# Softmax sums taken in the first pass over the scores, the logarithm folded into the second, eight heads to a mix

## The chip, the cores and the metric

The kernel runs on one core of a Trainium2 chip. The metric is the device time of one execution in microseconds. TensorE (PE) multiplies matrices, VectorE (DVE), ScalarE (ACT) and GpSimd (POOL) do elementwise work, SyncE (SP) issues transfers. PE writes its results to PSUM, eight banks of 512 float32 columns on 128 partitions; POOL reads and writes only SBUF.

## The reference, cut to what matters

A transformer layer on 16 items of 256 tokens and 512 features, all in float32: self-attention, cross-attention to a context of the same size, and a feed-forward part with 2048 hidden features. Each part starts with a layer norm whose scale and shift are computed from `cond`.

```python
def _attn(q, k, v):                       # 16 heads of 32 features, 256 queries, 256 keys
    scores = einsum('bqhd,bkhd->bhqk', q, k) * 32 ** -0.5
    out = einsum('bhqk,bkhd->bqhd', softmax(scores), v)
    return out.reshape(B, Lq, 512)
x = x + _attn(rope(q1), rope(k1), v1) @ sa_out_w.T      # q1, k1, v1 from adaln(x)
x = x + _attn(rope(q2), rope(k2), v2) @ ca_out_w.T      # q2 from adaln(x), k2, v2 from context
x = x + (gelu(adaln(x) @ ffn_w1.T + b1) @ ffn_w2.T + b2)
```

`rope` turns each pair of features (t1, t2) into (t1 cos - t2 sin, t2 cos + t1 sin).

## The kernel before

Accuracy is kept by splitting each float32 operand of a projection into a high part and a low part (`w_hi`, `w_lo`; `xx_hi`, `xx_lo`; `o_hi`, `o_lo`) and summing three products. ACT makes the high part by a copy, DVE or POOL subtracts to get the low part.

The two attention layers are one stage of 32 items (16 of self-attention, 16 of cross-attention), each of 16 heads, so 512 heads in a row; the feed-forward part is a second stage. The order of the attention stage is written out by hand in `stage_order`: `put(place, step)` gives every step a place, three places to a head, and every engine walks through the same list and does the steps that are its own. PE, ACT, DVE, POOL and SP therefore each work strictly in that order, and wait on semaphores for each other.

For every head n the list has two passes, eight heads (`LAG`) apart:

- `scores`: PE multiplies q by k into a bank of `ps_s` (L603, two products of 256 queries x 256 keys in halves of 128 queries), and DVE takes the negative maximum of each query over the keys (L851). Then the bank is free.
- `max_split`, `max_turn`, `max_copy`, once per four heads: DVE splits the maxima of four heads in a high and a low part (L859, L862), PE turns them by a product with the identity (L612), and ACT copies them into eight extra rows of `qT` (L729).
- `weigh`: PE computes the scores once more, transposed (keys on the partitions), with the negative maxima added by the extra rows (L623), ACT takes the exponential with the scale 32 ** -0.5 into `prob` (L737), and POOL adds the two halves of the keys into `sums_sb` (L908).
- `mix`, once per four heads (a "quad"): PE multiplies v by `prob` into the left half of the bank `ps_o` (L636) and a matrix of ones by `sums_sb` into its right half (L643), so that every row holds the softmax sum. `invert` (ACT, L744 and L746) turns the sum into its inverse by a logarithm and an exponential, `divide` (DVE, L867) multiplies, `o_split` (ACT, L753) and `o_low` (POOL, L896) split the result for the output projection.

Between these stand the projections of the items ahead, about two units per head: `project` (L589, L593), the turning of x with its modulation on ACT (`turn_x`, L692), and rope: DVE multiplies by cos (L822) and sin (L826), POOL adds (L902), ACT makes the high part (L722) and DVE the low part (`rope_low`, L843), and SP sends both through memory into the stacked layout of `qT` and `kT`.

`ps_s` has four banks, taken in turn by all steps of the kinds `scores`, `weigh` and `max_turn` in the order of the list (`score_users`); a step waits until the user four turns before it has been read (`scores_left`). `ps_g` has three banks and `ps_o` one. `prob` has room for six heads (`NP`).

## Time and profile before

| | |
|---|---|
| median of three runs | 1990.77 us (1989.99 to 1994.31) |
| span of the profiled execution | 1991.3 us |
| PE busy in the span | 1955.2 us, 98% |
| ACT busy | 1221.5 us, 61% |
| DVE busy | 1335.1 us, 67% |
| POOL busy | 1097.4 us, 55% |
| attention stage | up to about 1306 us |

The profiled execution has a time only as its span; it lies among the three timed runs, so the span is used as its own time. A row of a group names line, engine, operation, output<-input, shape and count, then the busy time in us and the mean ns of one, then the engine's idle time just before. Idle time of an engine that is not the bound costs nothing. Busy time counts overlapping instructions of an engine once; the mean ns is an instruction's whole length.

### The profile page before, as it was taken

What the parts mean: (1) busy time and instruction counts of PE and PEld (TensorE: products, weight loads), DVE (VectorE), ACT (ScalarE), POOL (GpSimd) and SP (SyncE); (2) the same over time, 40 slices, a digit from 0 to 9 for tenths busy, and PEclk for the clock granted to TensorE, in tenths of its full rate; (3) what the DMA queues carried; (4) which work ended last, traced back from release to release, by engine and by line L of the source; (5) the groups of instructions that cost most, each with busy time, mean ns of one, the idle gap of its engine ahead of it and who ended that gap; (6) DMA issues with size and microseconds to landing.
All of it is one profiled execution on the core that took longest, in us unless ns stands there. A gap on an engine that the chain in (4) does not pass through costs nothing. (4 is left out here: it accounts for less than half of the span.)

```text
span 1991.3 us, 40759 instructions
## 1 busy us (share of the span) xinstructions
PE 1955.2 (98%) x14612; PEld 1666.6 (84%) x14612; DVE 1335.1 (67%) x2317; ACT 1221.5 (61%) x2277; POOL 1097.4 (55%) x1205
## 2 busy tenths in 40 slices
PE   7999999999999999999999999899999999999999
PEld 6788888888887888888888887678998989989998
DVE  6866776776677676666667666545676676666654
ACT  3565566666666666666666666655656666666654
POOL 2555566566666676766666676523444363553531
PEclk9999999999999999999999999999999999999999
DMA  7877667676778686667667676543322323232230
GB/s 245 219 203 182 173 172 193 162 192 177 179 196 224 174 222 192 180 192 207 186 173 206 190 180 177 152 133 97 115 82 78 107 64 96 85 95 88 63 96 32
DMA packets 300197, 307.53 MB, mean 154 GB/s; under 512 B 15840, under 2 KB 253664, under 8 KB 300000
## 3 DMA queue, kind: packets, MB, share of 16 engines
q1 hardware_dynamic: 299408, 304.45, 55.4%
q8 instruction: 121, 1.98, 0.4%
q14 instruction: 76, 0.62, 0.1%
q10 hardware_dynamic: 592, 0.47, 0.1%
HBM read 212.59 MB, written 92.27 MB: 153 GB/s over the span
## 5 line engine op out<-in xcount | busy, mean ns | idle before, releaser
L908 POOL TENSOR_TENSOR sums_sb<-prob 128x256 f32<-128x256 f32 x512 | 405.1, 796 | 323.1 <-ACT prob L737 321.8
L851 DVE TENSOR_REDUCE neg_max<-ps_s 128x2 f32<-128x512 f32 x512 | 347.7, 686 | 335.2 <-PE ps_s L603 332.8
L737 ACT ACTIVATE prob<-ps_s 128x512 f32<-128x512 f32 x512 | 304.6, 596 | 348.6 <-PE ps_s L623 343.3
L902 POOL TENSOR_TENSOR rope_c<-rope_c,rope_s 128x512 f32<-128x512 f32 x128 | 179.0, 1398 | 115.9 <-DVE rope_s L826 115.1
L603 PE MATMUL ps_s<-kT,qT 96*128 96x256 f32 x1024 | 225.0, 301 | 2.3 <-DMA qT<-q_turned 2.3
L603 PEld LDWEIGHTS ps_s<-kT,qT 96*128 96x128 f32 x1024 | 164.5, 190 | 65.5 <-issue 53.9
L623 PE MATMUL ps_s<-qT,kT 104*128 104x256 f32 x1024 | 207.7, 284 | 10.0 <-ACT qT L729 7.2
L593 PE MATMUL ps_g<-xx_hi,w_hi 128*128 128x256 f32 x1024 | 210.4, 287 | 3.4 <-DVE rope_s L826 2.0
L593 PE MATMUL ps_g<-xx_hi,w_lo 128*128 128x256 f32 x1024 | 205.4, 282 | 0.0
L593 PE MATMUL ps_g<-xx_lo,w_hi 128*128 128x256 f32 x1024 | 204.8, 281 | 0.0
L1266 PE MATMUL ps_y<-w_hi,h_hi 128*128 128x512 f32 x512 | 201.5, 393 | 1.2 <-DVE h_lo L1391 1.2
L623 PEld LDWEIGHTS ps_s<-qT,kT 104*128 104x128 f32 x1024 | 170.6, 190 | 36.4 <-ACT qT L729 13.9
L1266 PE MATMUL ps_y<-w_lo,h_hi 128*128 128x512 f32 x512 | 200.6, 392 | 0.0
L1266 PE MATMUL ps_y<-w_hi,h_lo 128*128 128x512 f32 x512 | 199.4, 389 | 0.0
L1391 DVE TENSOR_TENSOR h_lo<-h_sb,h_hi 128x512 fp32r<-128x512 f32 x128 | 111.2, 872 | 103.7 <-ACT h_hi L1289 102.4
L1250 PE MATMUL ps_h<-xf_hi,cw_hi 128*128 128x256 f32 x592 | 167.4, 283 | 0.0
L1250 PE MATMUL ps_h<-xf_lo,cw_hi 128*128 128x256 f32 x592 | 165.8, 280 | 0.0
L1250 PE MATMUL ps_h<-xf_hi,cw_lo 128*128 128x256 f32 x592 | 165.7, 280 | 0.0
L593 PEld LDWEIGHTS ps_g<-xx_hi,w_hi 128*128 128x128 f32 x1024 | 158.4, 190 | 8.5 <-issue 5.2
L593 PEld LDWEIGHTS ps_g<-xx_lo,w_hi 128*128 128x128 f32 x1024 | 158.7, 191 | 0.0
L593 PEld LDWEIGHTS ps_g<-xx_hi,w_lo 128*128 128x128 f32 x1024 | 158.0, 190 | 0.0
L729 ACT ACTIVATE qT<-ps_s 8x1024 fp32r<-8x1024 f32 x128 | 130.4, 1018 | 3.1
(157 smaller groups left out, 4823.7 us busy)
## 6 DMA issues: line engine op xcount, KB each, us to landing
kT<-k_turned SPq DMA_DIRECT2D x192, 256.0 KB, 4.8
qT<-q_turned SPq DMA_DIRECT2D x64, 512.0 KB, 7.0
f_raw<-in_w1T SPq DMA_DIRECT2D x124, 256.0 KB, 3.1
k_turned<-rot_hi SPq DMA_DIRECT2D x64, 256.0 KB, 4.2
k_turned<-rot_lo SPq DMA_DIRECT2D x64, 256.0 KB, 4.3
q_turned<-rot_hi SPq DMA_DIRECT2D x64, 256.0 KB, 2.5
q_turned<-rot_lo SPq DMA_DIRECT2D x64, 256.0 KB, 2.6
qT<-q_turned SPq DMA_DIRECT2D x64, 256.0 KB, 7.5
```

The source lines that it names most:

```text
L593: ins = eng.matmul(ps_g[:, b, s * L:(s + 1) * L], w[:, row, (T * s + t) * P:(T * s + t + 1) * P], a[:, c, :], start=c == 0 and j == 0 and ...
L603: ins = eng.matmul(ps_s[:, score_bank(step), t * L:(t + 1) * L], qT[0:ROWS, G % NG, j, t * P:(t + 1) * P], kT[0:ROWS, G % NG, j, :], start ...
L623: ins = eng.matmul(ps_s[:, score_bank(step), t * L:(t + 1) * L], kT[:, G % NG, j, t * P:(t + 1) * P], qT[:, G % NG, j, :], start=True, sto ...
L729: eng.activation(qT[ROWS:MROWS, G % NG, OH * half:OH * (half + 1), :], ps_s[ROWS:MROWS, score_bank(step), 0:L].unsqueeze(1).broadcast_to([ ...
L737: eng.activation(prob[:, n % NP, :, :].rearrange("p t l -> p (t l)"), ps_s[:, score_bank(step), :], ACT.Exp, scale=HD ** -0.5).then_inc(ex ...
L851: eng.tensor_reduce(neg_max[G % 2][:, :, j], ps_s[:, score_bank(step), :].rearrange("p (t l) -> p t l", l=L), AX.X, ALU.max, negate=True). ...
L902: eng.tensor_tensor(rope_c[n % 2][:, :, :], rope_c[n % 2][:, :, :], rope_s[:, :, :], ALU.add).then_inc(rope_added, 1)
L908: eng.tensor_tensor(sums_sb[:, n % NP, :], prob[:, n % NP, 0, :], prob[:, n % NP, 1, :], ALU.add).then_inc(halves_added, 1)
L1250: ins = eng.matmul(ps_h[:, bank(p, n), 0:L], w[:, cols], x_[:, k, :], start=n in OPENS and k == 0 and j == 0, stop=k == 1 and j == 2, skip ...
L1266: ins = eng.matmul(ps_y[:, t, :], h[:, t * P:(t + 1) * P], w, start=c == 0 and j == 0, stop=c == FC - 1 and j == 2)
L1391: eng.tensor_tensor(h_lo[a % NH][:, :], h_sb[a % 2][:, :], h_hi[a % NH][:, :].bitcast(F32), ALU.subtract).then_inc(h_lo_done, 1)
```

## The change

The softmax sum is no longer taken from the second pass. A new ACT step `total` follows the maximum in the first pass: two exponentials of 128x256 (one for each half of the queries), read and written in place in the bank of `ps_s`, each with the negative maximum as a per-partition bias and with its sum over the keys written to `total`. The bank stays taken until they are done. Once per four heads ACT takes the logarithm of the sums (`log`), and DVE subtracts it from the negative maxima before it splits them (`max_split`, which now waits for `log` and stands three places later), so that the second pass gives normalized weights. The ones product, `sums_sb`, `invert` and `divide` are gone. A mix takes eight heads and one bank of `ps_s`, of which there are now five; `ps_o` is gone. `o_split` and `o_low` work once per eight heads on 128x512 and read that bank, so `o_low` moves from POOL to DVE. `rope_low` moves from DVE to POOL, and POOL's addition in rope becomes a subtraction and an addition of 128x256. The scale 32 ** -0.5 is put into the tables of cos and sin. `prob` has room for ten heads. Some projections, the store and the last items' steps move by one to five places. The modulation of x (L692) and the copies of the maxima (L729) are left as they are, on ACT.

```diff
-            late = {N: 24, N + 1: 14}.get(ahead, 0)
+            late = {N: 26, N + 1: 14}.get(ahead, 0)
...
-                turns(shares((p + 29, 6, k[:4]), (p + 45, 7, k[4:])))
+                turns(shares((p + 29, 6, k[:4]), (p + 46, 7, k[4:])))
...
-                    spread(p + 45, 7, v)
+                    spread(p + 46, 7, v)
...
-                    shares((p + 29, 6, v[:4]), (p + 45, 7, v[4:]))
+                    shares((p + 29, 6, v[:4]), (p + 46, 7, v[4:]))
...
-                turns(spread(p + 52, 14, q))
+                turns(spread(p + 53, 13, q))
...
-            spread(p + 36, 9, [("project", "o", i - 1, t, c) for cs in (range(KC - 1), (KC - 1,)) for t in range(T) for c in cs])
-            put(p + 47, "store", i - 1)
+            spread(p + 37, 9, [("project", "o", i - 1, t, c) for cs in (range(KC - 1), (KC - 1,)) for t in range(T) for c in cs])
+            put(p + 48, "store", i - 1)
...
-                spread(p + (58, 66, 78)[c], 6, [("project", "o", i, t, c) for t in range(T)])
+                spread(p + (58, 66, 83)[c], 6, [("project", "o", i, t, c) for t in range(T)])
...
         for half in range(2):
-            put(24 * G + 12 * half + 10, "max_split", G, half)
+            put(24 * G + 12 * half + 12, "log", G, half)
+            put(24 * G + 12 * half + 13, "max_split", G, half)
             put(24 * G + 12 * half + 19, "max_turn", G, half)
             put(24 * G + 12 * half + 20, "max_copy", G, half)
         if G:
             put(24 * G - 20, "stack", "k", G)
             put(24 * G - 17, "stack", "q", G)
 
-    for quad in range(4 * N):
-        place = 3 * (4 * quad + LAG + 5) + 2
-        for n, kind in enumerate(("mix", "invert", "divide", "o_split", "o_low")):
-            put(place + 2 * n, kind, quad)
+    for G in range(2 * N):
+        place = 3 * (8 * G + LAG + 9) + 2
+        for n, kind in enumerate(("mix", "o_split", "o_low")):
+            put(place + n, kind, G)
...
+            if part == 2 and n < HEADS:
+                yield ("total", n)
             for step in places.pop(3 * n + part, ()):
...
-    score_users = [step for step in order if step[0] in ("scores", "weigh", "max_turn")]
+    score_users = [step for step in order if step[0] in ("scores", "weigh", "max_turn", "mix")]
     score_turn = {step: n for n, step in enumerate(score_users)}
-    NS = 4
+    NS = 5
...
             cos_sb = sb("cos_sb", [P, L])
             pick_sb = sb("pick_sb", [P, OH])
...
@@ -375,14 +378,14 @@
             NV = 3
             v_sb = [sb(f"v_sb{n}", [P, T, D]) if n == (N_ITEMS - 1) % NV else v_kept[(N_ITEMS - 2 - n) % NV == 0] for n in range(NV)]
             neg_max = [sb(f"neg_max{n}", [P, T, HG]) for n in range(2)]
+            total = [sb(f"total{n}", [P, T, HG]) for n in range(2)]
+            log_sb = [sb(f"log_sb{n}", [P, T, OH]) for n in range(2)]
...
 
             max_parts = sb("max_parts", [P, T, MROWS])
-            NP = 6
+            NP = 10
             prob = sb("prob", [P, NP, T, L])
-            sums_sb = sb("sums_sb", [P, NP, L])
-            ones = sb("ones", [P, HD])
-
-            o_sb = sb("o_sb", [P, L])
+
             o_hi = sb("o_hi", [P, KC, L], F32R)
...
-                return {"scores": max_done, "weigh": exp_done, "max_turn": maxes_copied}[old[0]], nth[old]
+                return {"scores": total_done, "weigh": exp_done, "max_turn": maxes_copied, "mix": o_lo_done}[old[0]], nth[old]
...
                     elif kind == "mix":
-                        quad = step[1]
-                        i, c = divmod(quad, KC)
-                        eng.wait_ge(exp_done, OH * (quad + 1))
-                        if c == 0:
+                        G = step[1]
+                        i, g = divmod(G, 2)
+                        b = score_bank(step)
+                        eng.wait_ge(exp_done, HG * (G + 1))
+                        if g == 0:
                             eng.wait_ge(v_done, values[i, 1])
-                        if quad:
-                            eng.wait_ge(o_divided, quad)
-                        for k in range(T):
-                            for j in range(OH):
-                                ins = eng.matmul(ps_o[j * HD:(j + 1) * HD, 0, 0:L],
-                                                 v_sb[i % NV][:, k, c * P + j * HD:c * P + (j + 1) * HD],
-                                                 prob[:, (OH * quad + j) % NP, k, :], start=k == 0, stop=k == T - 1)
-                        if quad == 0:
-                            eng.wait_ge(ones_set, 1)
-                        eng.wait_ge(halves_added, OH * (quad + 1))
-                        for j in range(OH):
-                            ins = eng.matmul(ps_o[j * HD:(j + 1) * HD, 0, L:2 * L], ones[:, :],
-                                             sums_sb[:, (OH * quad + j) % NP, :], start=True, stop=True)
-                        ins.then_inc(mix_done, 1)
+                        for c in (2 * g, 2 * g + 1):
+                            cols = slice((c % 2) * L, (c % 2 + 1) * L)
+                            for k in range(T):
+                                for j in range(OH):
+                                    n = OH * (KC * i + c) + j
+                                    ins = eng.matmul(ps_s[j * HD:(j + 1) * HD, b, cols],
+                                                     v_sb[i % NV][:, k, c * P + j * HD:c * P + (j + 1) * HD],
+                                                     prob[:, n % NP, k, :], start=k == 0, stop=k == T - 1)
+                            ins.then_inc(mix_done, 1)
...
+                    elif kind == "total":
+                        n = step[1]
+                        G, j = divmod(n, HG)
+                        eng.wait_ge(max_done, n + 1)
+                        if j == 0 and G >= 2:
+                            eng.wait_ge(log_done, 2 * (G - 1))
+                        scores = ps_s[:, score_bank(("scores", n)), :]
+                        for t in range(T):
+                            ins = eng.activation(scores[:, t * L:(t + 1) * L], scores[:, t * L:(t + 1) * L], ACT.Exp,
+                                                 bias=neg_max[G % 2][:, t, j:j + 1], accum_out=total[G % 2][:, t, j:j + 1])
+                        ins.then_inc(total_done, 1)
+                    elif kind == "log":
+                        G, half = step[1:]
+                        eng.wait_ge(total_done, HG * G + OH * (half + 1))
+                        if nth[step] > 2:
+                            eng.wait_ge(shift_done, nth[step] - 2)
+                        eng.activation(log_sb[half][:, :, :], total[G % 2][:, :, OH * half:OH * (half + 1)], ACT.Ln).then_inc(log_done, 1)
                     elif kind == "weigh":
                         n = step[1]
                         eng.wait_ge(weigh_done, n + 1)
                         if n >= NP:
                             eng.wait_ge(mix_done, (n - NP) // OH + 1)
-                        eng.activation(prob[:, n % NP, :, :].rearrange("p t l -> p (t l)"), ps_s[:, score_bank(step), :], ACT.Exp,
-                                       scale=HD ** -0.5).then_inc(exp_done, 1)
-                    elif kind == "invert":
-                        quad = step[1]
-                        eng.wait_ge(mix_done, quad + 1)
-                        if quad:
-                            eng.wait_ge(o_lo_done, quad)
-                        eng.activation(o_sb[:, :], ps_o[:, 0, L:2 * L], ACT.Ln).then_inc(log_done, 1)
-                        eng.wait_ge(log_done, quad + 1)
-                        eng.activation(o_sb[:, :], o_sb[:, :], ACT.Exp, scale=-1.0).then_inc(den_inverted, 1)
+                        eng.activation(prob[:, n % NP, :, :].rearrange("p t l -> p (t l)"), ps_s[:, score_bank(step), :],
+                                       ACT.Exp).then_inc(exp_done, 1)
                     elif kind == "o_split":
-                        quad = step[1]
-                        i, c = divmod(quad, KC)
-                        eng.wait_ge(o_divided, quad + 1)
-                        if i and c == 0:
+                        G = step[1]
+                        i, g = divmod(G, 2)
+                        eng.wait_ge(mix_done, 2 * (G + 1))
+                        if i and g == 0:
                             eng.wait_ge(product_done, products["o", i - 1, 1])
-                        eng.activation(o_hi[:, c, :], o_sb[:, :], ACT.Copy).then_inc(o_hi_done, 1)
+                        eng.activation(o_hi[:, 2 * g:2 * g + 2, :], ps_s[:, score_bank(("mix", G)), :].rearrange("p (c l) -> p c l", l=L),
+                                       ACT.Copy).then_inc(o_hi_done, 1)
...
-                        eng.tensor_tensor(rope_s[:, :, :], pair[:, ::-1, :], sin_sb[:, :, :], ALU.mult).then_inc(rope_taken, 1)
+                        eng.tensor_tensor(rope_s[:, :, :], pair[:, ::-1, :], sin_sb[:, :].unsqueeze(1).broadcast_to([P, 2, L]),
+                                          ALU.mult).then_inc(rope_taken, 1)
...
-                    elif kind == "rope_low":
-                        n = ropes[step[1:]]
-                        if n > NT:
-                            eng.wait_ge(*rot_free(n))
-                        eng.wait_ge(rot_hi_done, n)
-                        eng.tensor_tensor(rot_lo[:, n % NT, :, :], rope_c[n % 2][:, :, :],
-                                          rot_hi[:, n % NT, :, :].bitcast(F32), ALU.subtract).then_inc(rot_lo_done, 1)
                     elif kind == "scores":
                         n = step[1]
                         G, j = divmod(n, HG)
@@ -855,19 +856,23 @@
                         eng.wait_ge(max_done, HG * G + OH * (half + 1))
                         if nth[step] > 1:
                             eng.wait_ge(max_turned, nth[step] - 1)
+                        eng.wait_ge(log_done, nth[step])
                         mine = neg_max[G % 2][:, :, OH * half:OH * (half + 1)]
-                        eng.tensor_reduce(max_parts[:, :, ROWS:ROWS + OH].bitcast(F32R), mine.unsqueeze(3), AX.X,
+                        eng.tensor_tensor(shift[:, :, :], mine, log_sb[half][:, :, :], ALU.subtract).then_inc(shift_done, 1)
+                        eng.wait_ge(shift_done, nth[step])
+                        eng.tensor_reduce(max_parts[:, :, ROWS:ROWS + OH].bitcast(F32R), shift[:, :, :].unsqueeze(3), AX.X,
                                           ALU.max).then_inc(max_hi_done, 1)
                         eng.wait_ge(max_hi_done, nth[step])
-                        eng.tensor_tensor(max_parts[:, :, ROWS + OH:MROWS], mine, max_parts[:, :, ROWS:ROWS + OH],
+                        eng.tensor_tensor(max_parts[:, :, ROWS + OH:MROWS], shift[:, :, :], max_parts[:, :, ROWS:ROWS + OH],
                                           ALU.subtract).then_inc(max_split, 1)
-                    elif kind == "divide":
-                        quad = step[1]
-                        eng.wait_ge(den_inverted, quad + 1)
-                        eng.tensor_tensor(o_sb[:, :], ps_o[:, 0, 0:L], o_sb[:, :], ALU.mult).then_inc(o_divided, 1)
+                    elif kind == "o_low":
+                        G = step[1]
+                        eng.wait_ge(o_hi_done, G + 1)
+                        chunks = slice(2 * (G % 2), 2 * (G % 2) + 2)
+                        eng.tensor_tensor(o_lo[:, chunks, :], ps_s[:, score_bank(("mix", G)), :].rearrange("p (c l) -> p c l", l=L),
+                                          o_hi[:, chunks, :].bitcast(F32), ALU.subtract).then_inc(o_lo_done, 1)
...
-                    elif kind == "o_low":
-                        quad = step[1]
-                        eng.wait_ge(o_hi_done, quad + 1)
-                        eng.tensor_tensor(o_lo[:, quad % KC, :], o_sb[:, :], o_hi[:, quad % KC, :].bitcast(F32),
-                                          ALU.subtract).then_inc(o_lo_done, 1)
                     elif kind == "project" and step[1] in "qk" and step[4] == KC - 1:
                         n = ropes[step[1:4]]
                         eng.wait_ge(cos_done, n)
                         eng.wait_ge(rope_taken, n)
-                        eng.tensor_tensor(rope_c[n % 2][:, :, :], rope_c[n % 2][:, :, :], rope_s[:, :, :], ALU.add).then_inc(rope_added, 1)
-                    elif kind == "weigh":
-                        n = step[1]
-                        eng.wait_ge(exp_done, n + 1)
-                        if n >= NP:
-                            eng.wait_ge(mix_done, (n - NP) // OH + 1)
-                        eng.tensor_tensor(sums_sb[:, n % NP, :], prob[:, n % NP, 0, :], prob[:, n % NP, 1, :],
-                                          ALU.add).then_inc(halves_added, 1)
+                        eng.tensor_tensor(rope_c[n % 2][:, 0, :], rope_c[n % 2][:, 0, :], rope_s[:, 0, :], ALU.subtract)
+                        eng.tensor_tensor(rope_c[n % 2][:, 1, :], rope_c[n % 2][:, 1, :], rope_s[:, 1, :], ALU.add).then_inc(rope_added, 1)
+                    elif kind == "rope_low":
+                        n = ropes[step[1:]]
+                        if n > NT:
+                            eng.wait_ge(*rot_free(n))
+                        eng.wait_ge(rot_hi_done, n)
+                        eng.tensor_tensor(rot_lo[:, n % NT, :, :], rope_c[n % 2][:, :, :],
+                                          rot_hi[:, n % NT, :, :].bitcast(F32), ALU.subtract).then_inc(rot_lo_done, 1)
...
-    cos = np.cos(ang).astype(np.float32)
-    sin = np.sin(ang).astype(np.float32)
-    return cos, np.stack([-sin, sin], 1)
+    by = (2 * half) ** -0.25
```

## Rows read from the trace of the kernel before

**Rows 1.** The page's first part: busy time, share of span, instructions.
```profile
PE 1955.2 (98%) x14612; PEld 1666.6 (84%) x14612; DVE 1335.1 (67%) x2317; ACT 1221.5 (61%) x2277; POOL 1097.4 (55%) x1205
```

**Rows 2.** Windows: stretch, length, busy of each engine (count), clock, DMA share, GB/s.
```profile
30.00:1306.00 1276.00, 1253.55 (x10288) 1043.21 (x10289) 880.20 (x1607) 804.25 (x1482) 807.26 (x896) 1.00 0.70 187
1306.00:1991.00 685.00, 679.20 (x4167) 605.46 (x4165) 435.06 (x671) 406.80 (x778) 282.75 (x299) 1.00 0.29 89
```

**Rows 3.** Longest of PE's waits, 30:1306: total us, times, longest us.
```profile
PE ps_s L623 <- ACT qT L729: 7.2, 8, 2.1
```

**Rows 4.** PE groups: busy us, mean ns | idle before.
```profile
L636 PE MATMUL ps_o<-prob,v_kept 128*32 128x256 f32 x1344 | 89.9, 385 | 0.0
L643 PE MATMUL ps_o<-sums_sb,ones 128*32 128x256 f32 x1024 | 79.3, 381 | 0.9 <-POOL sums_sb L908 0.9
```

**Rows 5.** Timeline of PE: start us, length us, instruction, count.
```profile
700.41 0.39 PE L589 MATMUL ps_g<-w_hi,xx_lo 128*128 128x512 f32 x1
700.73 1.07 PE L636 MATMUL ps_o<-prob,v_kept 128*32 128x256 f32 x16
701.62 0.61 PE L643 MATMUL ps_o<-sums_sb,ones 128*32 128x256 f32 x8
702.16 0.50 PE L603 MATMUL ps_s<-kT,qT 96*128 96x256 f32 x2
702.50 0.40 PE L589 MATMUL ps_g<-w_hi,xx_hi 128*128 128x512 f32 x1
```

**Rows 6.** ACT groups in 30:1306.
```profile
L737 ACT ACTIVATE prob<-ps_s 128x512 f32<-128x512 f32 x512 | 304.6, 596 | 348.6 <-PE ps_s L623 343.3
L729 ACT ACTIVATE qT<-ps_s 8x1024 fp32r<-8x1024 f32 x128 | 130.4, 1018 | 3.1
...
L746 ACT ACTIVATE o_sb<-o_sb 128x256 f32<-128x256 f32 x128 | 53.6, 418 | 4.0
L753 ACT ACTIVATE o_hi<-o_sb 128x256 fp32r<-128x256 f32 x128 | 53.4, 417 | 34.7 <-DVE o_sb L867 34.4
L744 ACT ACTIVATE o_sb<-ps_o 128x256 f32<-128x256 f32 x128 | 48.6, 379 | 1.3 <-PE ps_o L643 1.3
```

**Rows 7.** Timeline of ACT, one of its dense stretches.
```profile
705.51 1.02 ACT L729 ACTIVATE qT<-ps_s 8x1024 fp32r<-8x1024 f32 x1
706.55 0.60 ACT L715 ACTIVATE v_kept<-ps_g 128x512 f32<-128x512 f32 x1
707.04 0.59 ACT L737 ACTIVATE prob<-ps_s 128x512 f32<-128x512 f32 x1
707.52 0.42 ACT L753 ACTIVATE o_hi<-o_sb 128x256 fp32r<-128x256 f32 x1
```

**Rows 8.** ACT groups in 1306:1991 (the feed-forward stage).
```profile
L1294 ACT ACTIVATE u_sb<-ps_h 128x256 f32<-128x256 f32 x168 | 64.3, 383 | 83.0 <-PE ps_h L1250 81.7
...
L1371 ACT ACTIVATE h_sb<-ps_h,b_sb 128x256 f32<-128x256 f32 x56 | 26.4, 472 | 61.5 <-PE ps_h L1250 61.5
```

**Rows 9.** POOL groups.
```profile
L908 POOL TENSOR_TENSOR sums_sb<-prob 128x256 f32<-128x256 f32 x512 | 405.1, 796 | 323.1 <-ACT prob L737 321.8
L902 POOL TENSOR_TENSOR rope_c<-rope_c,rope_s 128x512 f32<-128x512 f32 x128 | 179.0, 1398 | 115.9 <-DVE rope_s L826 115.1 <-issue 0.3
L896 POOL TENSOR_TENSOR o_lo<-o_sb,o_hi 128x256 fp32r<-128x256 f32 x128 | 96.4, 753 | 2.0 <-ACT o_hi L753 2.0
L885 POOL TENSOR_TENSOR xx_lo<-xT,xx_hi 128x512 fp32r<-128x512 f32 x68 | 89.0, 1310 | 6.3 <-ACT xx_hi L701 6.3
```

**Rows 10.** DVE groups.
```profile
L851 DVE TENSOR_REDUCE neg_max<-ps_s 128x2 f32<-128x512 f32 x512 | 347.7, 686 | 335.2 <-PE ps_s L603 332.8
...
L843 DVE TENSOR_TENSOR rot_lo<-rope_c,rot_hi 128x512 fp32r<-128x512 f32 x128 | 106.2, 830 | 17.4 <-ACT rot_hi L722 17.4
...
L867 DVE TENSOR_TENSOR o_sb<-ps_o,o_sb 128x256 f32<-128x256 f32 x128 | 53.2, 416 | 8.9 <-ACT o_sb L746 8.8
...
L862 DVE TENSOR_TENSOR max_parts<-neg_max,max_parts 128x8 f32<-128x8 f32 x128 | 70.9, 554 | 4.4
```

31 lines of the change are left out of this document (15 added, 16 removed).

## The prediction

> **What bounds the kernel now.** I read the page's first part, then a table of windows by stage, then PE's waits, then the groups of PE and ACT and a few microseconds of both timelines. PE is busy for 98% of the span, and no other engine for more than 67% [rows 1]. In the attention stage, from 30 to 1306 us, PE is busy 1253.6 of 1276 us at a granted clock of 1.00, its upper level, 2.4 GHz, while ACT is busy 804 us and POOL 807 us [rows 2]. PE's waits there are small: the greatest in total is 7.2 us, for the copies of the maxima [rows 3]. So PE's stream of instructions sets the time, and only what leaves that stream can be gained, as long as no other engine becomes longer than what is left of it. The feed-forward stage of 685 us is not touched.
>
> **What PE saves.** The product with the ones goes: 512 products, 1024 instructions, 79.3 us busy [rows 4]. Busy time holds the last one's tail, which the next instruction covers, so I take starts: the eight instructions of a quad begin at 701.62 and the next one at 702.16, which is 0.54 us, times 128 quads = 69 us. The other part of the mix stays, but in 64 groups and not in 128. A switch between the 32-column products and the full ones costs something each time: before the mix the last projection starts at 700.41 and the mix at 700.73, 0.32 us later, and after it two score products take from 702.16 to 702.50, 0.34 us [rows 5]. The same instructions elsewhere in that stretch follow each other at about 0.23 us for each of these two steps, so a mix costs some 0.2 us in switches, and 64 fewer give 13 us. Together PE needs 69 + 13 = 82 us less. From the span of 1991.3 us that leaves 1909 us if nothing new waits. The span lies within the three timed runs, and 0.5 us above their median, so the two are taken as one.
>
> **What ACT gets.** This is where the change can lose. Now 804 us of busy time [rows 2]. Off: both parts of `invert` and the old `o_split`, 48.6 + 53.6 + 53.4 = 156 us [rows 6]. On: `o_split`, 64 of 128x512 out of PSUM at 0.60 us (the price of `prob`, [rows 6]) = 38 us. On: `log`, 128 of eight elements per partition. No row has so few; 128x256 takes 379 ns and 128x512 takes 596 [rows 6], so the part that doesn't grow with the columns is about 0.16 us. `log` must also see its own engine's sums finished, so I take 0.25 us, 32 us in all, with 20 as the lower end. That makes 804 - 156 + 38 + 32 = 718 us without the new exponentials.
>
> A dense engine does better than the mean lengths say, because neighbours overlap: in a dense stretch `v_kept` starts at 706.55, `prob` at 707.04 and the next at 707.52, so an instruction of 0.60 us occupies 0.49 us, 0.11 less than its length. The copy of the maxima does not share in this: 1.02 us long, next start after 1.04 us [rows 7]. Some 960 of the remaining ACT instructions could overlap by 0.11 us, 106 us at most; part of it is in the 804 already. I take 50 us more off: 668 us.
>
> The new exponentials: 1024 of 128x256 out of PSUM with a per-partition bias. Such a bias is seen in the feed-forward stage: 472 ns with it, 383 ns for a copy of the same size without it [rows 8]. Less the overlap, 0.36 us each. Writing out the sum is not seen anywhere in this trace. From below it costs nothing; from above it is a short instruction of its own without any overlap, 0.16 us, and the exponential then loses its own 0.11 too. I take 0.08 us, between nothing and 0.16, since the rows show that short fixed parts are mostly overlapped. So 1024 x 0.44 = 451 us, between 1024 x 0.36 = 369 and 1024 x 0.63 = 645.
>
> ACT then needs 668 + 451 = 1119 us, between 1037 and 1363 (718 + 645), in a stage in which PE needs 1276 - 82 = 1194 us. That is 94%: ACT does not become the bound at my value, but it comes near it.
>
> The Trainium skill (ScalarE: Activation LUTs, section What ACT_TABLE_LOAD costs) states 186 ns + 0.833 ns per element for an ACTIVATE, 93 ns more for a per-partition pointer operand, and an overlap of 93 ns back to back. The difference of 89 ns between the two rows agrees; by its figures an exponential would occupy 400 ns where the rows give 362, and by that estimate ACT would need 39 us more.
>
> **What the near-full ACT costs PE.** A bank of `ps_s` is now held through maximum and total. With five banks and the order scores, weigh, scores, weigh, the bank of scores n is wanted again by the weigh step 2.5 heads later. A head takes 1194 / 512 = 2.33 us, so 5.8 us. The path needs about 0.4 us of PE, 0.69 of DVE [rows 10] and two exponentials, 0.9: 2.0 us. That leaves 3.8 us for queues on ACT and DVE. In a plain stretch this is enough. But the modulation of x comes in clusters (four of L692, two splits, some 3 us of ACT in about 5 us), and a copy of the maxima of 1.04 us stands every four heads; behind these `prob` and `total` are late, then the bank, then PE. I estimate 0.7 us for each of 34 such clusters, 24 us in all. An ACT 30 us less loaded would have nearly none, one at 98% perhaps twice as many. So PE's waits in the stage grow from some 20 us to some 45.
>
> **The other edits.** `max_split` now waits for `log`; behind it on DVE stand the next heads' maxima and the rope products. The sums of four heads are ready about 2.8 us after the last head's scores, `log` 0.3 later, and PE wants the turn ten places, 7.6 us, after those scores: hidden by the projections between, at the price of part of a microsecond per item if that cover went. The extra subtraction is a DVE instruction like L862, at most 0.55 us, 128 times, 71 us. DVE loses `divide`, 53 us, and `rope_low`, 106, and gets `o_low`, 64 x 0.69 = 44 [rows 10]: 880 - 159 + 44 + 71 = 836 us, 70%, not the bound. POOL loses 405 and 96 us, and gets `rope_low` at 1.31 us, 168 us, and 0.2 us more for each rope, 25 us [rows 9]: about 500 us. A rotated tile is ready 0.2 + 0.5 us later; the stacking transfers start places later, and PE shows no greater wait than the 7.2 us above, so it stays hidden. The mix in a bank of `ps_s` holds it for some 4 us of 4.5 before it is wanted; small cost, in the 24 us. The moved projections add no work. The smaller sin table and the tables' scale cost nothing.
>
> So the sum: 1991.3 - 69 - 13 + 24 = 1933 us.
>
> **The rivals.** Cases and chances:
>
> (a) The forecast, 1918 to 1957 us: 0.42.
>
> (b) All of it is kept. Reading out the sums is free and ACT at 1037 us is 87% full; five banks are deep enough. 1991.3 - 82, plus up to 9 us: 1909 to 1918 us. For it: PE lost only 7 us to ACT so far. Against it: ACT had 37% idle then. 0.20.
>
> (c) ACT is just the bound: 1242 to 1271 us in the stage. It would come from a read-out of 0.16 us with the exponential's overlap kept, 668 + 1024 x 0.52 = 1200 us of work, and 42 to 71 us in which ACT itself waits: `o_split` stands one place behind its mix now, where the old one stood six behind, and each of the 64 mixes takes PE about 2 us. Time 1991.3 - 1276 + 1242 to 1271 = 1957 to 1986 us: 0.15.
>
> (d) The other side: ACT is the bound and slower than PE was. Place: `total`. Price: two exponentials per head at full length, with a read-out that overlaps nothing, 1.26 us per head, ACT at 1363 us, and the time 1991.3 + 87 = 2078 us. It decides when `total` costs more than (1276 - 668) / 512 = 1.19 us per head, 0.59 for each exponential with its read-out. For it: no row shows the read-out. Against it: it takes 0.23 us on top of 0.36. With bubbles around `log` less is enough, so 0.20.
>
> (e) No change, ACT as long in the stage as PE was, 1987 to 1995 us: 0.03.
>
> **How the numbers follow.** A measurement of this kernel tells about 0.2%, 4 us, from no change. Faster by more: (a) + (b) + nearly all of (c) = 0.77; within: 0.03; slower: 0.20. The likeliest case gives 1933 us. The range runs from (b)'s lower end, 1906 with room for the switch estimate, to 1988, the end of (c), and leaves out (d).
>
> **What the profile after would show.** Right: no L643-like product; the mix in 64 groups; PE busy in the stage near 1172 us and its waits on ACT (`total`, `prob`, maxima copies) 20 to 50 us; ACT busy about 1100 us; exponentials of `total` near 0.45 to 0.48 us; POOL near 500 us. The stage would end near 1248 us. Wrong: ACT over 97% busy with PE waiting over 60 us for it (c, d), an exponential with read-out over 0.59 us (d), PE's waits under 10 us (b), or PE's clock below 1.00 in the stage because of its new waits, which would make each of its instructions longer.

## The result, and the profile after

The changed kernel is slower by 1.1%: 2012.86 us median (2011.91 to 2015.55) against 1991.3 us, ratio 1.0106, 95% interval 1.0092 to 1.012. The prediction was 1933 us, in a range that ended at 1988.

First the page's first part after the change, which answers to [rows 1], and ACT's busy share in tenths in 40 slices of the span.

```profile
PE 1915.1 (95%) x13588; PEld 1655.2 (82%) x13588; DVE 1223.6 (61%) x2253; ACT 1585.5 (79%) x4133; POOL 782.8 (39%) x820
...
ACT  3799889998999999999999998955566566665654
```

Windows of the changed kernel: the attention stage, which now ends at 1326 us, its middle 500 us, and three stretches of 50 us. The columns are those of [rows 2].

```profile
30.00:1326.00 1296.00, 1214.56 (x9267) 1032.81 (x9266) 768.59 (x1544) 1168.36 (x3338) 493.30 (x510) 0.99 0.70 184
...
650.00:1150.00 500.00, 480.50 (x3739) 414.23 (x3738) 301.39 (x614) 472.26 (x1354) 214.25 (x221) 1.00 0.72 192
...
50.00:100.00 50.00, 39.46 (x268) 33.44 (x269) 32.03 (x62) 36.13 (x108) 17.29 (x18) 0.93 0.86 229
600.00:650.00 50.00, 45.12 (x332) 38.60 (x331) 34.95 (x63) 44.67 (x123) 21.55 (x21) 0.97 0.85 233
1200.00:1250.00 50.00, 41.04 (x302) 34.75 (x302) 27.89 (x52) 44.48 (x132) 14.41 (x16) 0.90 0.62 155
```

The stage is 20 us longer, PE's busy time in it 39 us shorter, and ACT's 364 us greater; in the middle 500 us ACT is busy for 94%. PE's idle time in the stage is 1296 - 1214.56 = 81 us, before it was 1276 - 1253.55 = 22. The middle of the kernel before, for comparison:

```profile
650.00:1150.00 500.00, 499.50 (x4122) 416.32 (x4121) 343.39 (x635) 322.51 (x596) 341.46 (x375) 1.00 0.71 194
```

The feed-forward stage is as long as before. So all of the loss, and all of the gain that did not come, is in the attention stage. Who PE waits for, total, times and longest; this answers to [rows 3].

```profile
PE ps_s L624 <- ACT qT L726: 25.4, 50, 1.2
PE ps_s L624 <- ACT ps_s L737: 24.6, 32, 1.8
PE ps_s L604 <- ACT ps_s L737: 8.5, 9, 2.1
```

There are two releasers: the copies of the maxima (7.2 us before, now 25.4) and the banks held by the new exponentials (L737), 33 us. In the middle 500 us alone the copies are the greater of the two:

```profile
PE ps_s L624 <- ACT qT L726: 12.3, 14, 0.9
PE ps_s L624 <- ACT ps_s L737: 6.0, 13, 0.5
```

**Where in the stage.** The copies of the maxima come once per four heads, 128 times, and so serve as milestones. The view of one line gives the first and the last start; the first row is of before, the second of after.

```profile
L729 ACT ACTIVATE qT<-ps_s x128: 1016/1018/1022, 62.3 to 1294.8; 8x1024 fp32r<-8x1024 f32 x128
```

```profile
L726 ACT ACTIVATE qT<-ps_s x128: 1017/1019/1024, 70.2 to 1313.2; 8x1024 fp32r<-8x1024 f32 x128
```

The first comes 7.9 us later, the last 18.4. In the timelines the 13th starts at 183.25 before and 192.68 after (9.4 later), and the 115th at 1181.26 and 1191.06 (9.8 later). So, against the kernel before, the loss is at the start and in the last tenth. Over the 102 intervals between, four heads take (1181.26 - 183.25) / 102 = 9.78 us before and 9.79 after: there PE's saving was eaten to the last digit. This interval is used below as the rate of the middle.

### The profile page after: what moved, and what is told of

It is laid out like the page before. It is cut to its first block and busy times, and to the rows that moved or that the text cites. A ratio compares the mean times of both kernels' runs of the same rounds, so it can differ in the third digit from the quotient of the medians.

```text
span 2010.2 us, 39605 instructions
## 1 busy us (share of the span) xinstructions
PE 1915.1 (95%) x13588; PEld 1655.2 (82%) x13588; DVE 1223.6 (61%) x2253; ACT 1585.5 (79%) x4133; POOL 782.8 (39%) x820
## 5 line engine op out<-in xcount | busy, mean ns | idle before, releaser
L852 DVE TENSOR_REDUCE neg_max<-ps_s 128x2 f32<-128x512 f32 x512 | 351.9, 688 | 283.2 <-PE ps_s L604 282.8
L737 ACT ACTIVATE ps_s<-ps_s,neg_max 128x256 f32<-128x256 f32 x1024 | 463.2, 457 | 22.8 <-DVE neg_max L852 22.5
L624 PE MATMUL ps_s<-qT,kT 104*128 104x256 f32 x1024 | 217.4, 294 | 53.8 <-ACT qT L726 25.4
L902 POOL TENSOR_TENSOR rope_c<-rope_c,rope_s 128x256 f32<-128x256 f32 x128 | 98.6, 770 | 432.9 <-DVE rope_s L833 432.9
L604 PE MATMUL ps_s<-kT,qT 96*128 96x256 f32 x1024 | 220.6, 297 | 15.0 <-ACT ps_s L737 8.5
L604 PEld LDWEIGHTS ps_s<-kT,qT 96*128 96x128 f32 x1024 | 170.3, 191 | 65.8 <-issue 25.1
L737 ACT ACTIVATION_READ_ACCUMULATOR ps_s<-ps_s,neg_max 128x1 f32 x1024 | 221.9, 217 | 0.0
L594 PE MATMUL ps_g<-xx_hi,w_hi 128*128 128x256 f32 x1024 | 215.3, 292 | 5.5 <-DVE rope_s L833 3.4
L909 POOL TENSOR_TENSOR rot_lo<-rope_c,rot_hi 128x512 fp32r<-128x512 f32 x128 | 165.6, 1294 | 64.4 <-ACT rot_hi L719 64.2
```

What stands on the lines that cost most here:

```text
L594: ins = eng.matmul(ps_g[:, b, s * L:(s + 1) * L], w[:, row, (T * s + t) * P:(T * s + t + 1) * P], a[:, c, :], start=c == 0 and j == 0 and ...
L604: ins = eng.matmul(ps_s[:, score_bank(step), t * L:(t + 1) * L], qT[0:ROWS, G % NG, j, t * P:(t + 1) * P], kT[0:ROWS, G % NG, j, :], start ...
L624: ins = eng.matmul(ps_s[:, score_bank(step), t * L:(t + 1) * L], kT[:, G % NG, j, t * P:(t + 1) * P], qT[:, G % NG, j, :], start=True, sto ...
L737: ins = eng.activation(scores[:, t * L:(t + 1) * L], scores[:, t * L:(t + 1) * L], ACT.Exp, bias=neg_max[G % 2][:, t, j:j + 1], accum_out= ...
L852: eng.tensor_reduce(neg_max[G % 2][:, :, j], ps_s[:, score_bank(step), :].rearrange("p (t l) -> p t l", l=L), AX.X, ALU.max, negate=True). ...
L902: eng.tensor_tensor(rope_c[n % 2][:, 0, :], rope_c[n % 2][:, 0, :], rope_s[:, 0, :], ALU.subtract)
```

## The experiments

The edits are shown against the changed kernel, except where it says that the kernel before is the base. Ratios are to the kernel before, on the same chip.

**The first pass without its exponentials.** The logarithm is taken of ones, so the output is not normalized.

```diff
-                    elif kind == "total": ...
-                        eng.wait_ge(total_done, HG * G + OH * (half + 1))       # in "log"
+                        eng.wait_ge(max_done, HG * G + OH * (half + 1))
-                return {"scores": total_done, ...
+                return {"scores": max_done, ...
```

> The changed kernel without the exponentials of the first pass: the bank is free after the maximum again, and the logarithm is taken of sums that are set to one, so the output is not normalized. ACT loses about 460 us. If the ones product and half of the mixes were worth the 82 us of the sum, and only the new ACT work takes them away, this gives 1908 to 1918 us. If PE's saving itself was mis-sized, or the eight-head mix in a score bank costs the gain, it stays above 1930.

Measured: 1935.86 us, ratio 0.9721 (0.9707 to 0.9736). The new exponentials cost 2012.86 - 1935.86 = 77 us, where the sum had 24. But the time is also 18 to 28 us above the expected 1908 to 1918, so PE's own terms were too good as well. The middle rate is (1123.68 - 183.88) / 102 = 9.21 us. Of the 77 us, 9 are lost up to the 13th copy, 59 from there to the 115th and 10 behind it. The middle of the stage reads:

```profile
650.00:1150.00 500.00, 494.42 (x3924) 430.10 (x3923) 319.80 (x642) 309.78 (x552) 225.90 (x232) 0.99 0.76 203
```

**The exponentials without the sums.** Output not normalized.

```diff
-  bias=neg_max[G % 2][:, t, j:j + 1], accum_out=total[G % 2][:, t, j:j + 1])
+  bias=neg_max[G % 2][:, t, j:j + 1])
```

> The changed kernel with both exponentials of the first pass but without their sums: the logarithm is taken of ones, the output is not normalized. ACT loses 1024 read-outs of about 0.09 us, some 90 us, and nothing in the order or in who waits for whom changes. Theory load (ACT has too little slack, its work makes the banks late): most of the 82 us comes back, 1935 to 1960 us. Theory order (DVE stands behind the logarithm and the maxima behind it come late) and theory chain (maximum and two exponentials hold a bank too long): much less than the load theory, 1985 to 2005 us.

Measured: 1975.61 us, 0.992 (0.9905 to 0.9935), middle rate 9.51 us. Taking about 92 us off ACT (0.09 us each, seen below) gives 37 us back, though the order and the chain of waits are the same. It lies between the two expectations and decides for neither: a bank is also held 0.18 us less in every head.

**The split of the maxima three places later.**

```diff
-            put(24 * G + 12 * half + 13, "max_split", G, half)
+            put(24 * G + 12 * half + 16, "max_split", G, half)
```

> The changed kernel with the split of the maxima three places later, behind the maximum of one more head, so that DVE does not stand behind the logarithm so early. No work changes. Theory order: DVE's 161 us of waiting for the logarithm shrink, the maxima come sooner and the time falls by 20 us or more, below 1990. Theory load: within 5 us of the changed kernel, 2008 to 2018 us, or slower since the turn of the maxima has three places less.

Measured: 2011.79 us, 1.0103 (1.0088 to 1.0118): no difference from the changed kernel. DVE's wait for the logarithm, the second largest in its list, is nearly gone, and the time is the same. The first row is of the changed kernel, the second of this run.

```profile
DVE shift L861 <- ACT log_sb L745: 161.4, 80, 3.3
```

```profile
DVE shift L861 <- ACT log_sb L745: 18.6, 16, 1.3
```

So that wait costs nothing here, and the theory of order falls.

**The modulation of x on DVE.**

```diff
-  ins = eng.activation(xT[:, k, :], ps_g[...], ACT.Identity, bias=gb[...], scale=gb[...])
+  ins = eng.tensor_scalar(xT[:, k, :], ps_g[...], gb[... scale], gb[... shift], ALU.mult, ALU.add)
```

> The changed kernel with the modulation of x (136 instructions of 128x256, 71 us busy) on DVE in place of ACT, at the same places of the order. Theory load: every us taken off ACT gives back about as much until PE is the bound, so 1950 to 1965 us, the more so as this work stands in clusters. Theory order: DVE gets later, 2005 us or above.

Measured: 1987.54 us, 0.9977 (0.9967 to 0.9986). 25 us back for 71 us off ACT. That is outside both expectations: less than the load theory's by 22 us or more, and faster than the changed kernel, where the order theory had it no better. No bank of `ps_s` is held shorter here and the order is the same, so this part of the loss is ACT's load.

**The copies of the maxima on DVE, and both.**

```diff
-  eng.activation(qT[ROWS:MROWS, ...], ps_s[ROWS:MROWS, ...].broadcast_to(...), ACT.Copy)
+  eng.tensor_copy(qT[ROWS:MROWS, ...], ps_s[ROWS:MROWS, ...].broadcast_to(...))
```

> The changed kernel with the copies of the maxima (128 of 8x1024, 1.02 us each, which overlap nothing on ACT) on DVE. ACT loses about 146 us, DVE gets about 155 us and is some 75% full. Load theory, by what the two runs before gave (0.27 us per four heads for 0.72 us of read-out, 0.19 for 0.55 us of modulation): 0.3 to 0.55 us per four heads, 1945 to 1975 us. If ACT's load were not the cause but the chain from maximum to copied maxima (log, split, turn, copy in ACT's and DVE's order), the gain is there only if DVE is free when the turn is done, and DVE's queue makes the maxima late: 1990 us or above.

> The changed kernel with both the modulation of x and the copies of the maxima on DVE. ACT loses about 217 us and is near 78% full, DVE gets 210 us and is near 82% full. Load theory: PE is the bound through the middle of the stage, the gain per four heads comes near the 0.57 us of the run without the first pass's exponentials, 1940 to 1955 us. If DVE then takes ACT's part as the one whose queue makes banks late: above 1960.

Measured: 1981.97 us, 0.9951 (0.9935 to 0.9968), and both 1978.33 us, 0.9924 (0.9907 to 0.994). The first lies between its two expectations; the second is above 1960, the case in which DVE takes ACT's part. The modulation adds only 4 us to the copies. PE now waits 22 us for the copies on DVE. With both, the middle of the stage reads:

```profile
650.00:1150.00 500.00, 486.38 (x3834) 421.16 (x3833) 398.26 (x735) 408.72 (x1281) 222.84 (x229) 1.00 0.76 200
```

ACT at 82%, DVE at 80%, and PE still loses 13.6 of 500 us.

**One exponential per head, nothing moved.** To tell DVE's price from ACT's: ACT loses as much as by both moves (407 us busy in the middle 500, where both moves leave 409), DVE gets nothing. Output not normalized.

```diff
-  for t in range(T):
-      ins = eng.activation(<half t>, <half t>, ACT.Exp, bias=..., accum_out=...)
+  ins = eng.activation(scores, scores, ACT.Exp, scale=0.01)
```

> The changed kernel with one exponential of 128x512 per head in the first pass, without bias and sums, in place of the two with sums; the logarithm is taken of ones, the output is not normalized. ACT loses about 0.41 us per head, 210 us, as much as in the run that moved the modulation and the copies to DVE (1978 us), but DVE gets nothing. Load theory: near the run without any first-pass exponential (1936 us), 1936 to 1950 us, and the 30 to 40 us to the run with both moved are DVE's price. If the length of the hold of a bank is the cause, with ACT's load of no account: it lies in proportion, half of the way between 1936 and 2013, 1965 us or above.

Measured: 1956.71 us, 0.9825 (0.981 to 0.9839), between the expectations. The same relief of ACT is worth 56 us when DVE gets nothing and 35 us when DVE gets the work. So the loaded DVE costs 22 us at most; part of them can be the shorter hold of a bank, which only this run has. In order of work taken off ACT (0, 92, about 210, about 461 us) the time is 2013, 1976, 1957, 1936 us: 0.40 us per us for the first step, 0.16 for the next, 0.08 for the last. There is no point at which the waits end; they thin out. Every step of this series also shortens the hold of a bank, and these runs don't part that from load.

**The kernel before, with the two exponentials and sums added.** The sums are not used. Four banks, as before.

```diff
+            if part == 2 and n < HEADS:
+                yield ("total", n)
-                return {"scores": max_done, ...
+                return {"scores": total_done, ...
```

> The kernel before the change with the first pass's two exponentials and their sums added, in place in the bank, and nothing done with the sums; all else, the product with the ones included, stays. ACT gets about 460 us on its 804 in 1276. Load theory: ACT is now the bound, at 1220 to 1270 us of work plus its own waits in the stage, so 2020 to 2060 us. If only the longer hold of a bank counted, with four banks: any value, but then ACT would stand idle for more than 10% of the stage.

Measured: 2153.52 us, 1.0806 (1.079 to 1.0822), above the load theory's 2020 to 2060 us. Its middle and its first wait:

```profile
650.00:1150.00 500.00, 467.14 (x3693) 376.03 (x3692) 312.61 (x582) 448.29 (x1277) 308.31 (x334) 1.00 0.66 178
```

```profile
PE ps_s L627 <- ACT ps_s L742: 100.5, 125, 2.9
```

ACT is 90% busy and not full, while PE waits 100 us for the held banks: here the load theory alone is not enough. ACT and PE, with four banks between them, stand idle by turns; that this is most of the miss is argued and not shown. The runs don't give the price of the fifth bank by itself.

**The low part of rope back on DVE**, in the changed kernel and in the one without the first pass's exponentials.

```diff
 def attention_vector:
+                    elif kind == "rope_low": ... eng.tensor_tensor(rot_lo..., ALU.subtract)
 def attention_gpsimd:
-                    elif kind == "rope_low": ...
```

> The changed kernel with the low part of rope back on DVE, where it was before. The first copy of the maxima came 7.9 us later than before the change, and also 5.8 us later without the first pass's exponentials. If the longer rope chain on POOL causes that, this run gets 4 to 8 us of it back at the start, 2004 to 2008 us. If the start is late for another reason, it stays at 2012 us; if DVE's load matters in the middle of the stage, it gets slower.

> The run without the first pass's exponentials (1936 us), with the low part of rope back on DVE. If the start's delay by the rope chain on POOL is a cost of its own, 6 to 9 us less, 1927 to 1930 us. If not, 1936 us.

Measured: 2004.18 us, 1.0058 (1.0043 to 1.0073), and 1924.07 us, 0.9656 (0.964 to 0.9672): 8.7 and 11.8 us less than their bases. In the first the start of the first copy goes from 70.2 to 64.6 us, and the middle rate stays at 9.79: that loss is at the start. In the second the first copy comes 4.3 us earlier (68.1 to 63.8) and the middle rate falls too, from 9.21 to 9.17, some 5 us over the 102 intervals: with ACT unloaded, rope's low part on POOL costs a little there as well.

**The kernel before without the product with the ones.** The inverse is taken of the bank's left half; output not normalized; waits and sums stay.

```diff
-                        for j in range(OH):
-                            ins = eng.matmul(ps_o[j * HD:(j + 1) * HD, 0, L:2 * L], ones[:, :], ...)
```

> The kernel before the change without the product with the ones, and with the inverse taken of something else in its place (the left half of the bank), so the output is not normalized; POOL's sums, the waits and ACT's work stay. By the sum's first term 69 us less: 1921 to 1925 us. If the product is worth less because other waits come to light when PE is shorter: 1930 to 1945 us.

Measured: 1948.37 us, 0.9776 (0.976 to 0.9792): 44 us, not 69, and so not the first term of the sum as it stood. The timeline of PE in this kernel shows a part of why:

```profile
700.64 1.07 PE L636 MATMUL ps_o<-prob,v_sb 128*32 128x256 f32 x16
701.64 0.51 PE L603 MATMUL ps_s<-kT,qT 96*128 96x256 f32 x2
```

From the mix to the next instruction are 1.00 us, where before the mix and the ones product together took 701.62 - 700.73 + 0.54 = 1.43 [rows 5]. So the product is worth 0.43 us, 55 us in 128 quads. The 0.54 us that the sum took held 0.11 us which stay when the mix itself is the last 32-column product. PE's waits for the copies of the maxima rise from 7.2 to 10.5 us; the rest of the 11 us between 55 and 44 is not itemized.

**Towards a better kernel.** The first run moves the copies and only the first eight low parts to DVE, the second the modulation too; the third is the first with the turn and copy of the maxima two places earlier, the fourth the second with the same.

```diff
+                    elif kind == "rope_low" and ropes[step[1:]] <= 8:      # on DVE, the others on POOL
-            put(24 * G + 12 * half + 19, "max_turn", G, half)
-            put(24 * G + 12 * half + 20, "max_copy", G, half)
+            put(24 * G + 12 * half + 17, "max_turn", G, half)
+            put(24 * G + 12 * half + 18, "max_copy", G, half)
```

> The changed kernel with the copies of the maxima on DVE (1982 us alone) and the low parts of the first eight rotated tiles on DVE, the others on POOL as in the change. If the 8 us of the run with all low parts on DVE come from the start alone, both add: 1973 to 1976 us. If they came from the middle of the stage: 1980 us or above.

> The same with the modulation of x on DVE too (1978 us with the two moves alone): 1968 to 1973 us if the start's 8 us add.

> The changed kernel with the copies of the maxima on DVE, the first eight low parts on DVE, and the turn and the copy of the maxima two places earlier (17 and 18 in place of 19 and 20), so that the second pass finds them sooner; no work changes. PE waited 22 us, 33 times, for these copies when they were on DVE. If that wait costs what it shows: 10 to 20 us less than the run with the two moves, 1955 to 1965 us. If it only takes the place of a wait for a bank that would come next: within 5 us of it, 1970 to 1978 us.

> The changed kernel with modulation and copies on DVE, the first eight low parts on DVE, and the turn and copy of the maxima two places earlier. Turning earlier gave 4 us where only the copies were on DVE. If DVE is the queue that is late now, its split is not ready at the earlier turn and it gives nothing or loses: 1966 to 1972 us. If the copies' lateness is what PE waits for: 1958 to 1964 us.

Measured: 1975.98 us (0.9921, 0.9904 to 0.9937), 1967.82 (0.9879, 0.9865 to 0.9894), 1972.13 (0.9901, 0.9887 to 0.9916) and 1959.63 us, 0.9832 (0.9818 to 0.9847). The first lands where both gains add, the second 0.2 us below that range; the third is within 5 us of its base, so there the wait for the copies only took the place of another; the fourth is in the range given for late copies. The last beats both kernels, by 32 us and by 53. The earlier turn gives 4 us where the copies alone are on DVE and 8 us with the modulation there too. In the last one the wait for a copy on DVE is down from the second run's 22.2 us to 3.6, and the turn waits for the split instead:

```profile
PE ps_s L613 <- DVE max_parts L872: 10.4, 8, 3.0
```

## Why the prediction was wrong

The result is the sum of three terms, each measured by a difference of runs: from 1992 us, 68 off (everything but the exponentials, with rope's low part on DVE: 1924.07), 12 on (low part on POOL: 1935.86), 77 on (exponentials and sums: 2012.86). The two losses are split in this order; the other way round rope's low part costs 9 and the exponentials 80.

**What PE saves.** Right in kind, too large: 82 us predicted, 68 measured. The first term was too large: the product with the ones was 55 us of starts and not 69, since part of a switch was counted with it, and 44 us of time. The second was too small. One mix of 32 instructions takes 1236.65 - 1234.79 = 1.86 us to the next start, where two of sixteen, as in the kernel without the ones product, take 2.00; with the 0.2 us of the two switches beside a mix that is 0.34 us, 22 us in 64, where the sum had 13. By time, all of the change but the exponentials takes the kernel without the ones product from 1948 to 1924 us, 24 more.

```profile
1234.79 1.93 PE L639 MATMUL ps_s<-prob,v_kept 128*32 128x256 f32 x32
1236.65 0.50 PE L604 MATMUL ps_s<-kT,qT 96*128 96x256 f32 x2
```

**What ACT gets.** The price in dispute, that of an exponential with its sum, was right. The timeline of ACT after the change:

```profile
701.84 0.44 ACT L737 ACTIVATE ps_s<-ps_s,neg_max 128x256 f32<-128x256 f32 x1
702.20 0.20 ACT L737 ACTIVATION_READ_ACCUMULATOR ps_s<-ps_s,neg_max 128x1 f32 x1
702.29 0.45 ACT L737 ACTIVATE ps_s<-ps_s,neg_max 128x256 f32<-128x256 f32 x1
```

Exponential to read-out 0.36 us, read-out to the next 0.09: 0.45 us where 0.44 was taken, 461 us in all where the sum had 451. ACT's busy time in the stage is 1168 us where 1119 was expected; what is left without the exponentials is 707 us, not 668, and the run without them has 725. The 50 us of further overlap did not come: 718 us without them was nearer.

**What the near-full ACT costs PE.** This step failed, and it decided the sign: 24 us predicted, 77 measured. The mis-sized term is "0.7 us for each of 34 such clusters". PE's own starts show where it loses. The turns of the maxima (PE, L613) come four to an item and cut it into quarters; these are the mean times from turn to turn over 25 items, from the 13th turn on. The modulation of x stands on both sides of the first quarter's beginning.

| quarter | 1st | 2nd | 3rd | 4th | an item |
|---|---|---|---|---|---|
| changed kernel, us | 11.40 | 9.45 | 9.33 | 9.02 | 39.2 |
| without the exponentials, us | 10.07 | 8.80 | 9.26 | 8.75 | 36.9 |
| lost, us | 1.33 | 0.65 | 0.07 | 0.27 | 2.3 |
| ACT busy, changed kernel | 96% | 90% | 88% | 97% | |

"In a plain stretch this is enough", said the prediction, and that held: the third quarter, with ACT 88% busy, loses 0.07 us. What an item loses, it loses at the cluster and behind it, 2.3 us where 0.7 was taken, and 32 times 2.3 is 74 of the 77 us. The prediction had the path right (late `total`, late bank, late PE) and its length wrong. Around the cluster ACT is 96 to 97% busy, and what is late there comes back at two places of every item. One is a bank, 17.6 us in 26 waits between the 13th and the 115th copy. The other, some 8 us later, is a copy of the maxima, 20.2 us in 38 waits; that one had no price of its own in the sum. One item's two places in PE's timeline:

```profile
713.09 0.40 PE L594 MATMUL ps_g<-xx_lo,w_hi 128*128 128x256 f32 x2
713.97 0.51 PE L624 MATMUL ps_s<-qT,kT 104*128 104x256 f32 x2 [0.48 <-ACT ps_s L737]
714.31 0.40 PE L590 MATMUL ps_g<-w_hi,xx_hi 128*128 128x512 f32 x1
...
721.66 0.47 PE L624 MATMUL ps_s<-qT,kT 104*128 104x256 f32 x2 [0.92 <-ACT qT L726]
```

A wait costs more than it shows. Before the first one 713.97 - 713.09 = 0.88 us pass from start to start where 0.24 is usual, and behind it 0.34: together 0.74 us for a wait shown as 0.48, since the rest counts as busy. In the middle 500 us PE is idle for 19.5 us, against 0.5 before and 5.6 without the exponentials.

The sum also took the bank as wanted again after 2.5 heads, 5.8 us. The list of the banks' users holds the turns and the mixes too, (512 + 512 + 128 + 64) / 512 = 2.4 users a head, so five banks come round in 2.1 heads, 4.9 us. In the middle a head holds its bank for 3.1 us in the mean from the start of its maximum (2.7 in the median), but the two heads of each item behind the cluster hold it for 5.5 and 4.9.

ACT is not simply the bound there: it has waits of its own, the greatest for PE's second-pass scores, and a microsecond taken off it gives back 0.4 and not 1. Both engines have a fixed order, and neither can use the time in which it waits.

```profile
ACT prob L751 <- PE ps_s L624: 58.8, 94, 3.7
```

How much of the 2.3 us is ACT's load and how much the longer hold of a bank stays open. Load alone is shown for a part: moving the modulation off ACT, with every hold and place as it was, gives 25 us back, and the first quarter falls from 11.40 to 10.54 us.

The Trainium skill (ScalarE: Activation LUTs, section What ACT_TABLE_LOAD costs) would have put ACT 39 us higher than the forecast by its 93 ns for a pointer operand and the same for overlap. The trace gives 0.36 us to the read-out where it gives 0.40, so it does not agree in size, though the load it gives, 1158 us, is nearer to the 1168 measured.

**The other edits.** "It stays hidden" was wrong for rope: its low part on POOL cost 9 to 12 us, most of it at the start, where there is nothing ahead to hide a longer rotation. The price of the instructions was right: `rope_low` on POOL takes 1.29 us where 1.31 was taken. That DVE behind the logarithm costs little was right.

**The clock.** The prediction named a clock below 1.00 as a sign against it. It came in part: 0.93, 0.97 and 0.90 of full in the three stretches above, some of their time at the lower level of 1.2 GHz, where the same stretches of before show 1.00, 1.00 and 0.97. In the worst one PE was busy only 41 of 50 us. But the mean is 0.992 against 0.993 without the exponentials (0.999 before), and that run shows 0.93, 0.97 and 0.93 in the same stretches, so the clock is next to no part of the 77 us. It may be in the 68 and the 12, and was not tried by itself.

**The rivals.** (b) fell. The forecast (a) has its mechanism, not its size. (d) has its sign but not its cause: the read-out did not cost too much. (c) and (e) gave ACT the length of the stage, which it did not have, 1168 of 1296 us. What happened is (a)'s cluster at three times its price, on a saving of PE that was 14 us smaller, and rope's 12 us: 53 + 14 + 12 is 79 of the 80 us between forecast and result. In the last tenth the loss against the kernel before grows from 9.8 to 18.4 us; without the exponentials nothing is lost there (57.6 us ahead of before at the 115th copy, 58.7 at the last), at the same granted clock of 0.94. That it is for want of projections between the heads is argued and not shown. ACT's load is not all of it: from the 115th copy to the last the changed kernel takes 122.1 us, the one with both moves to DVE 122.9, the one without the exponentials 112.5. The cause of this part stays open.

## What to carry to other kernels

When two engines walk through fixed orders and hand a few buffers to and fro, look at the second engine's load where its work bunches and not at its mean: here 94% in the mean was 97% around the cluster, and PE lost three times what was charged for the cluster, while the quarter with 88% lost next to nothing. Follow the backlog to every point at which the first engine waits for the second; here a copy 8 us on cost as much as the bank. Count all users of a ring of buffers before saying when one is wanted again. A saving on the bound is read best from starts with the part taken out in mind, so that a switch which stays is not counted with it. A longer chain that is hidden in the middle is bare at the start, and a big entry in the list of waits of an engine that is no bound (161 us here) may be worth nothing.

## What the runs showed of the hardware

A read-out of ACT's sums is an instruction of its own, 217 ns long in the mean, but it takes only 0.09 us of ACT's time. The exponential in place in PSUM, with a bias, is 457 ns long.

A DVE instruction with operands in SBUF can be several times longer while POOL works. The scaling of x is the same instruction in both kernels, 827 ns before and, with POOL busy for 493 us of the stage and not 807:

```profile
L789 DVE TENSOR_SCALAR xn<-xn,mv,rstd 128x512 f32<-128x512 f32 x68 | 37.5, 554 | 1.1 <-POOL rstd L884 1.1
```

The split of the maxima went from 554 ns [rows 10] to 175:

```profile
L866 DVE TENSOR_TENSOR max_parts<-shift,max_parts 128x8 f32<-128x8 f32 x128 | 22.4, 175 | 4.4
```

That is not POOL's total load, since without the first pass's exponentials POOL is as little busy and the same split takes 325 ns. It is the meeting of the two. In the kernel before, the 49 splits that meet no POOL instruction take 0.17 us each, and the 67 that lie wholly under POOL's work 0.86 us in the mean, up to 1.18. One of them ends within 0.03 us of the POOL instruction over it; the last row meets none.

```profile
687.16 1.29 POOL L902 TENSOR_TENSOR rope_c<-rope_c,rope_s 128x512 f32<-128x512 f32 x1 [1.60 <-DVE rope_s L826]
687.46 1.02 DVE L862 TENSOR_TENSOR max_parts<-neg_max,max_parts 128x8 f32<-128x8 f32 x1
...
697.73 0.17 DVE L862 TENSOR_TENSOR max_parts<-neg_max,max_parts 128x8 f32<-128x8 f32 x1
```

It is not only POOL's sums that do it: the instruction here is rope's addition.
